# Graph layer on one core: group 0's first layer ahead of chunk 1's pick, chunk 1's sort batches in later steps

## The reference

```
edge_in = concatenate([h[row], h[col], dist])      # row = src, col = dst
e = silu(edge_in @ eW1 + eb1)                      # first layer, 129 -> 128
e = silu(e @ eW2 + eb2)                            # second layer, 128 -> 128
agg = segment_sum(e, row, num_segments=3125)
out = silu(concatenate([h, agg]) @ nW1 + nb1) @ nW2 + nb2
result = layernorm(x + out)
```

## Time and profile before

| | us |
|---|---|
| median of three runs | 621.68 (620.03 to 623.82) |
| profiled execution, its own time | 620.83 |
| its span, first to last instruction | 619.0 |
| PE busy | 564.6 (91%) |
| POOL busy | 427.4 (69%) |
| DVE busy | 427.0 (69%) |
| ACT busy | 367.1 (59%) |

### The profile page before, as it was taken

How to read it: one execution, slowest core, us unless ns; L and a number is a source line. 1 busy time by engine, 2 the same in 40 slices (tenths; PEclk the granted TensorE clock), 3 DMA queues, 4 the chain that set the end, 5 groups by cost and what they waited for, 6 DMA issues and landing times.

```text
span 619.0 us, 15895 instructions
## 1 busy us (share of the span) xinstructions
PE 564.6 (91%) x5003; PEld 485.2 (78%) x5003; DVE 427.0 (69%) x1317; ACT 367.1 (59%) x831; POOL 427.4 (69%) x463
## 2 busy tenths in 40 slices
PE   5998899999999999999999999999987898879795
PEld 4676587888897898888878987888876777779683
DVE  7987799799679888778777777777643442224256
ACT  4448486645656666665655565556556565657464
POOL 2355477777777777777777777777777777777740
PEclk9887799989989999999999899989999999989998
DMA  5311111111112112111111111111112112111111
GB/s 123 105 39 35 34 54 57 52 54 56 52 52 57 52 53 57 53 54 52 56 52 56 55 52 56 55 53 53 55 52 57 53 52 56 52 55 55 52 39 52
DMA packets 17219, 34.23 MB, mean 55 GB/s; under 512 B 8133, under 2 KB 9352, under 8 KB 17017
## 3 DMA queue, kind: packets, MB, share of 16 engines
q0 software_dynamic: 14080, 28.86, 16.3%
q1 hardware_dynamic: 2748, 4.20, 2.5%
q10 hardware_dynamic: 314, 0.16, 0.1%
HBM read 30.73 MB, written 2.40 MB: 54 GB/s over the span
## 4 chain that ended last, share of the span: by engine, by line
POOL 38%; PE 32%; issue 15%; DVE 12%; ACT 1%; DVEq 1%; DMA 1%; POOLq 0%; ACTq 0%
POOL q_rows L839 37%; PE layer_ps L852 14%; PE sort_ps L852 10%; PE seg_ps L852 6%; DVE count L1250 1%; PE turn_ps L1015 1%; DVE load_hot L1399 1%; DVE agg L1511 1%; DVE col_hot L1394 1%; DMA q_rows<-q_table,q_index 1%; DVEq L1503 1%; DVE hot L1496 1%; DVE load_hot L1438 1%; ACT p_table L619 1%; DVE count L1294 1%
## 5 line engine op out<-in xcount | busy, mean ns | idle before, releaser
L839 POOL DMA_INDIRECT q_rows<-q_table,q_index x440 | 417.9, 950 | 150.9 <-issue 132.0
L688 ACT ACTIVATE e<-layer_ps 128x512 f32<-128x512 f32 x110 | 65.6, 597 | 198.7 <-PE seg_ps L852 187.7
L1511 DVE TENSOR_TENSOR agg<-agg,seg_ps 128x125 f32 x416 | 93.4, 281 | 113.7 <-PE seg_ps L852 111.3
L852 PE MATMUL layer_ps<-hotT,p_table 128*128 128x128 bf16 x1320 | 159.3, 227 | 0.3
L852 PE MATMUL layer_ps<-ident_f,q_rows 128*128 128x128 f32 x440 | 128.0, 291 | 25.9 <-DMA q_rows<-q_table,q_index 24.9
L852 PEld LDWEIGHTS layer_ps<-hotT,p_table 128*128 x1320 | 123.4, 100 | 22.2 <-issue 2.6
L852 PE MATMUL seg_ps<-hot,e 128*128 128x125 f32 x880 | 124.4, 285 | 3.8 <-DVE agg L1511 3.7
L852 PE MATMUL layer_ps<-w_sb,h 128*128 128x128 f32 x880 | 123.3, 284 | 0.0
L852 PEld LDWEIGHTS layer_ps<-w_sb,h 128*128 128x128 f32 x880 | 111.9, 196 | 4.6
L852 PEld LDWEIGHTS seg_ps<-hot,e 128*128 128x128 f32 x880 | 109.1, 195 | 5.9 <-issue 3.8
L852 PEld LDWEIGHTS layer_ps<-ident_f,q_rows 128*128 128x128 f32 x440 | 64.0, 146 | 34.5 <-DMA q_rows<-q_table,q_index 32.9
(11 more groups left out here) (223 smaller groups left out, 511.5 us busy)
## 6 DMA issues: line engine op xcount, KB each, us to landing
q_rows<-q_table,q_index POOLq DMA_INDIRECT x440
q_table<-q_in_sb SPq DMA_DIRECT2D x1, 896.0 KB
x_sb<-in_x_dram SPq DMA_DIRECT2D x1, 700.0 KB
q_table<-q_in_sb SPq DMA_DIRECT2D x1, 504.0 KB
out_dram<-x_sb SPq DMA_DIRECT2D x2, 224.0 KB
out_dram<-x_sb SPq DMA_DIRECT2D x1, 252.0 KB
w_in<-in_edge_weight_dram SPq DMA_DIRECT2D x1, 185.9 KB
dst_i<-in_dst_dram SPq DMA_DIRECT2D x1, 185.9 KB
```

Of the source, the lines that this page charges most:

```text
L688: A.activation(e2[:, m % 2, :], e_of(m)[:], ACT.Silu).then_inc(e2_ready, 1)
L839: P.indirect_dma_start(q_rows[:, g % RING, j, :], None, q_table, bass.IndirectOffsetOnAxis(ap=q_index[:, GT * g + j:GT * g + j + 1], axis= ...
L852: return nc.tensor.matmul(o, lhsT, rhs, start=start, stop=stop, **kw)
L1511: D.tensor_tensor(o, o, seg_ps[:, j * LO:(j + 1) * LO], ALU.add).then_inc(agg_added, 1)
```

## The change

In ScalarE's program the copy of chunk 2's first spread bank moves from before the loop into step 0, behind `put_bias(0)`. In TensorE's program `first_layer(0)` comes ahead of `turn(2)`, chunk 1's PICK and DEST, and `spread_windows(2, 0)` moves from before the loop to behind them. In the plan chunk 1's five sort batches on TensorE move from step 1 to steps 2 (two) and 3 (three), CLOSE of chunk 1 from step 1 to step 3, and DVE's WINDOW of chunk 1 from behind the first sort batch of `VECTOR[0]` to behind the second. The number of instructions stays as it is.

```
 def plan():
     at(TENSOR, 0, (CARRY, 1, 0), (SPREAD, 2, 1))
-    sorts(1, [0, 0, 0, 1, 1], [1, 1, 1, 1, 1])
-    VECTOR[0].insert(1, (WINDOW, 1, 0))
-    at(TENSOR, 1, (CLOSE, 1, 0))
+    sorts(1, [0, 0, 0, 1, 1], [2, 2, 3, 3, 3])
+    VECTOR[0].insert(2, (WINDOW, 1, 0))
+    at(TENSOR, 3, (CLOSE, 1, 0))
...
             load_twice(0, COL0[1], ECOL)
-            copy_spread(2, 0)
             for m in range(GROUPS):
...
                     put_bias(m + 1)
+                if m == 0:
+                    copy_spread(2, 0)
...
             turn(1).then_inc(hotT_ps_ready, 1)
-            spread_windows(2, 0)
             for m in range(GROUPS):
                 if 2 <= m <= TIGHT:
                     second_layer(m - 2)
-                if m == 0:
-                    turn(2).then_inc(hotT_ps_ready, 1)
-                    pick(1)
-                    part(DEST, 1, 0)
                 last = first_layer(m)
...
                 if m <= TIGHT:
                     last.then_inc(step_ready, 1)
+                if m == 0:
+                    turn(2).then_inc(hotT_ps_ready, 1)
+                    pick(1)
+                    part(DEST, 1, 0)
+                    spread_windows(2, 0)
```

## The result

The changed kernel takes 627.14 us (median of five runs, 625.97 to 628.11) against 622.46 us (620.03 to 623.82) for the kernel before on the same chip: the ratio is 1.0088, 95% interval 1.0066 to 1.0110. It is slower, by 4.7 us between the medians and by 5.5 us by the ratio. The profiled executions stand 6.3 us apart (627.14 and 620.83, spans 625.3 and 619.0), because the profiled one of before lies 1.6 us under its median. What follows compares the profiled executions.

A forecast was written before the change was run, and what follows sets the result against it. POOL's gather stream was taken to set the end. PE late at step 4 by 6.9, plus 1.2 for clock, less 0.6 of room, gave +7.5 us: 628.7 us, range for 8 in 10 622.7 to 632.5.

The forecast's parts named there:

- the first hole: POOL's 5.21 us idle ahead of group 4: it goes, a gain of 4.5 us for the moment.
- the new 3.35 us wait for ACT's copy: PE in step 0, ahead of spread (2, 1): it stands 3 us until ACT's copy ends at 63.1.
- 5.54 us of idle PE ahead of OFFSET: Chunk 2's OFFSET directly behind CLOSE: PE idles 5.2 us for DVE's total, until 85.9, and is 6.9 us late.
- The putting of WINDOW one batch later: On DVE, chunk 1: costs nothing, since DVE would wait there; 2.0 us of idle time turns into work.
- The term that was mis-sized: Step 3's chain through PE, DVE and ACT: CLOSE of chunk 1 ends at about 80.6, before the change at 73.72.
- The clock after the hole: PE's work behind the idle time ahead of chunk 2's OFFSET may run at half clock: taken as +1.2 us.
- The term of 2.5: Upper end of the clock loss behind PE's idle time ahead of OFFSET, 2.5 us; the time would be 1.3 us longer.
- rival C: Much slower: half clock after both holes and again later, +11.7 us, 632.5 to 633.4; chance 10%.
- The room at group 27: PE's first layer there can be only 0.6 us late before POOL's gather of group 31 is late.
- A: Faster: POOL's two holes go, group 8 is gathered 5.2 us earlier, time 615.6 us; chance 10%.
- B: No measurable change: the clock rises early, all links at their low end, +1.9 us, 622.7 to 623.5; chance 15%.
- D: Waits not taken as read, at spread (2, 1) or OFFSET: +2 to +4 us; chance 5%.

The follow-up runs named there:

- r5_after: The changed kernel with five ring slots for the gathered rows instead of four: 624.73 us, 1.0048 of the kernel before.
- e3: The changed kernel with chunk 2's OFFSET moved from step 3 to step 4 and what follows it one step later: 629.59 us, 1.0118 of the kernel before.
- e4: The changed kernel with spread (2,0) and ScalarE's copy of it back ahead of the loop: 626.12 us, 1.0079 of the kernel before.
- e2: The kernel before with only the changed plan (sorts, CLOSE, WINDOW), TensorE's and ScalarE's order as it was: 623.26 us, 1.0034 of the kernel before.
- e1: The changed kernel's TensorE and ScalarE order with the plan of the kernel before (five sorts and CLOSE in step 1): 625.71 us, ratio 1.0073.

## Why the prediction was right

**The mechanism** was right at every link, and both of the signs that would have refuted it stayed away (OFFSET at 84.33 and not before 82, the last gather at 603.59 and not before 599): the first hole gone (56.30, I had 55.8), the new 3.35 us wait for ACT's copy (I had 3.0), the hole back at group 5 (66.64; 66.0), batch 4 released by PE, turn(5) held by ACT and DVE's one-hots, 5.54 us of idle PE ahead of OFFSET, group 8 waiting for a first layer (89.72; 88.6 or later), small waits of POOL for PE at groups 11 to 31. The putting of WINDOW one batch later cost nothing: DVE's idle time ahead of it is 1.26 us.

**The size** was too large. The forecast was +7.5 us for POOL's stream, from two starting points 628.3 and 629.2, of which it took 628.7. The stream moved by 6.0 at group 31, the profiled execution by 6.3, the medians by 4.7. That 627.14 lies as near to 628.7 as it does is in part luck: the kernel before, measured twice more with it, has its median at 622.46 and not at 621.68. The term that was mis-sized is CLOSE: I put it at 80.6, it ended at 78.8, so OFFSET came 5.4 us late and not 6.9. I had taken half clock until step 2 was over; the clock rose at about 68 us (0.84 from 66 to 72), so that the second layer, the first layer, the turn and two batches of step 2 ran from 66.99 to 71.4. The first of these batches, which I had until 72.5, released DVE's batch 4 at 70.78.

**The clock after the hole** was +1.2 in the sum. First layer 4 starts 6.64 us late and OFFSET 5.37: 1.3. The row for 84 to 88 us shows 0.50, with PE idle from 78.8 to 84.3 before it. The Trainium skill, "TensorE: Matmul & The Clock Gate", section "HAM oscillation — how this bites in real kernels", says that such holes put the array back at half rate, and this trace agrees. The term of 2.5 that I had joined to it was too large: the clock was back at full while first layer 4 ran (its last matmuls took 0.33 us for three, the first 0.53). First layer 4 ends 7.3 us late, and by first layer 5 it is 6.0, since PE's 0.68 us wait for DVE ahead of the pick was gone, the 0.7 that the prediction had. Its own figures would have made the upper end 3.5 - 0.7 = 2.8; it wrote 2.5 there and 2.3 in rival C. The low clock after 54 us, which it took as agreement, stood behind holes of 0.90, 0.86 and 0.57 us, so it was weaker evidence than this hole of 5.54.

**The room at group 27** was 0.6 in the sum and 0.67 in the changed kernel, and 0.6 to 0.7 in all seven variants with four slots.

**The rivals.** A (faster) fails where I had it: PE regained nothing from 76 to 220 us (first layer 4 starts 6.6 us late, first layer 27 6.7). With five slots the change is no gain either, see r5_after. B (+1.9) is excluded: the interval's low end, 1.0066, is +4.1 us. C (half clock in the last sorts too, and again later) did not happen in the changed kernel. In e3 and e4 those sorts did run largely at half clock (4.09 and 4.14 us), and even so the ratios stay at 1.0118 and 1.0079, +7.3 and +4.9 us and not +11.7. D (the waits not as read) is excluded: both stand in the trace, 3.35 us ahead of spread (2, 1) and 5.54 us ahead of OFFSET.

## What to carry to other kernels

When a kernel's busiest engine and the engine whose stream sets the end are two, look for the place where a ring couples them, and read the room there: a delay upstream costs what exceeds it. One more buffer gave 3.6 us here. It doesn't make the delay harmless: look for the next road by which it arrives, here the row numbers of a later chunk, and compare each version with and without the buffer. When work moves to a later step, look at what was already there: here the next chunk's first part, which had two steps between itself and what it waits for, came to stand directly behind it. Taking away one wait in a chain through three engines gives little as long as another engine's chain runs beside it. And before a difference between two profiled executions is put down to an edit, see whether it begins ahead of the first instruction that the edit moves, as in e3.

## What the runs showed of the hardware

A removed wait was returned as clock. In e4 PE stood 1.3 us longer ahead of turn(5), and the same 18 matmuls took 4.14 us and not 2.66. The other profiled executions go the same way: behind waits of 1.62 us (changed kernel) and 1.65 (e2) these matmuls took 2.66 us, behind 2.17 (e3) 4.09. Each is one execution, so it is a pattern and not proof.

In e1 PE's clock fell to 0.78 and 0.65 in 84 to 96 us though PE was busy 11.2 of those 12 us. The fall came while it ran the 125x5 float32 matmuls of the pick, from 86.08 on, and the second layer behind them took 2.08 us where it takes 1.16 at full clock. The kernel before ran the same work there at 1.00 and fell later, to 0.83 in 120 to 130, behind the next pick. Why one fell and the other did not isn't shown. In e1 it made PE's lateness grow from 2.5 us at first layer 4 to 4.7 at first layer 7.
